# A recommender tower on one core: another order for the first chunks, rotation loads of 120 partitions, rows stored five times

## The reference, cut to what matters

```python
e = jnp.stack([tbl_f[ids[:, f]] for f in range(39)], axis=1)        # (512, 39, 16)
x0 = xk = e
for idx, (W, b) in enumerate(params):                                # W: (39, fk, 128), fk = 39, 64, 64
    z = relu(jnp.einsum('bhd,bkd,hks->bsd', x0, xk, W) + b[None, :, None])
    if idx != 2:
        xk = z[:, :64, :]; direct.append(z[:, 64:, :])
    else:
        direct.append(z)
z = jnp.sum(jnp.concatenate(direct, axis=1), axis=-1)                # (512, 256)
h = concat([z, dense_ctx], 1); h = relu(h @ W_top1 + b_top1); h = relu(h @ W_top2 + b_top2)
y = h @ W_top3
```

## Time and profile before

| | us |
|---|---|
| median of 3 runs (704.96 to 708.79) | 708.59 |
| profiled execution, its own time | 708.69 |
| span of the profiled execution | 706.9 |
| PE busy | 635.9 (90%) |
| DVE busy | 601.0 (85%) |
| POOL busy | 351.6 (50%) |
| ACT busy | 244.8 (35%) |
| DMA, share of 16 engines, SP's queue | 60.7% |

### The profile page before, as it was taken

How to read it: one execution, slowest core, us unless ns; L and a number is a source line. 1 busy time by engine, 2 the same in 40 slices (tenths; PEclk the granted TensorE clock), 3 DMA queues, 4 the chain that set the end, 5 groups by cost and what they waited for, 6 DMA issues and landing times.

```text
span 706.9 us, 5986 instructions
## 1 busy us (share of the span) xinstructions
PE 635.9 (90%) x1856; PEld 347.7 (49%) x1856; DVE 601.0 (85%) x548; ACT 244.8 (35%) x315; POOL 351.6 (50%) x391
## 2 busy tenths in 40 slices
PE   0142679999999999999999999999999999999998
PEld 0020335555555555555555555555555555555544
DVE  0220768999999999999999999999999999999920
ACT  0210242434434434343443334344344343432312
POOL 6765045374756657464746464747566222132210
PEclk9985698999999999999999999999999999999999
DMA  8587087959586776859494949494867668070100
GB/s 204 102 295 168 12 225 230 279 146 251 157 231 194 165 258 143 286 127 301 106 316 89 302 103 278 128 265 142 232 194 189 228 150 275 30 268 1 61 0 0
DMA packets 95118, 126.05 MB, mean 178 GB/s; under 512 B 30312, under 2 KB 38222, under 8 KB 95087
## 3 DMA queue, kind: packets, MB, share of 16 engines
q1 hardware_dynamic: 87935, 124.32, 60.7%
q0 software_dynamic: 5120, 1.32, 2.3%
q10 hardware_dynamic: 2032, 0.04, 0.2%
HBM read 123.09 MB, written 6.39 MB: 183 GB/s over the span
## 4 chain that ended last, share of the span: by engine, by line
PE 83%; DMA 7%; DVE 4%; SPq 3%; issue 1%; POOL 1%; ACT 1%; DVEq 0%; ACTq 0%
PE z L575 53%; PE z L565 9%; PE z L566 8%; PE z L567 8%; DMA rot<-fields 3%; DMA bc<-fields 2%; DVE low L491 1%; POOL emb L309 1%; DMA fields<-xt 1%; DVE whole L515 1%; DVE raw L507 1%; PE z L582 1%; PE z L583 1%; PE z L635 1%; SPq L241 1%
## 5 line engine op out<-in xcount | busy, mean ns | idle before, releaser
L575 PE MATMUL z<-whole,w 128*128 128x512 f32 (+2 forms) x928 | 433.4, 600 | 31.2 <-DVE whole L515 30.4
L575 PEld LDWEIGHTS z<-whole,w 128*128 128x128 f32 (+2 forms) x928 | 177.0, 192 | 188.0 <-issue 172.1
L388 ACT ACTIVATE high<-raw 128x1024 fp32r<-128x1024 f32 (+1 forms) x128 | 135.3, 1058 | 363.4 <-DVE raw L507 312.0
L515 DVE TENSOR_TENSOR whole<-bc,xk 128x1024 f32<-128x1024 f32 (+1 forms) x208 | 229.6, 1127 | 6.7 <-issue 2.4
L309 POOL DMA_INDIRECT emb<-in_tables,rows_all x160 | 194.9, 1218 | 54.1 <-issue 52.9
L491 DVE TENSOR_TENSOR low<-raw,high 128x1024 fp32r<-128x1024 f32 (+1 forms) x128 | 162.0, 1266 | 0.7 <-ACT high L388 0.7
L565 PE MATMUL z<-high,w_high 128*128 128x512 f32 (+1 forms) x256 | 141.8, 554 | 19.2 <-DVE low L491 19.1
L507 DVE TENSOR_TENSOR raw<-bc,xk 128x1024 f32<-128x1024 f32 x112 | 135.5, 1210 | 0.0
L327 POOL TENSOR_TENSOR stack<-stack_raw,stack 64x512 fp32r<-64x512 f32 x32 | 44.6, 1393 | 180.5 <-ACT stack L395 179.6
L566 PE MATMUL z<-high,w_low 128*128 128x512 f32 (+1 forms) x256 | 102.6, 401 | 0.0
L567 PE MATMUL z<-low,w_high 128*128 128x512 f32 (+1 forms) x256 | 102.4, 400 | 0.0
(11 more groups left out here) (52 smaller groups left out, 162.3 us busy)
## 6 DMA issues: line engine op xcount, KB each, us to landing
bc<-fields SPq DMA_DIRECT2D x64, 1024.0 KB, 8.5
rot<-fields SPq DMA_DIRECT2D x32, 390.0 KB
bc<-fields SPq DMA_DIRECT2D x16, 768.0 KB
rot<-fields SPq DMA_DIRECT2D x48, 156.0 KB
rot<-fields SPq DMA_DIRECT2D x16, 312.0 KB
bc<-fields SPq DMA_DIRECT2D x32, 128.0 KB
rep<-fields SPq DMA_DIRECT2D x48, 78.0 KB
fields<-fields SPq DMA_DIRECT2D x16, 234.0 KB
```

The lines of the kernel that those rows point to most:

```text
L388: act.activation(high[0:m, k % PART_SLOTS], raw[0:m, k % RAW_SLOTS], ACT.Copy).then_inc(high_ready, 1)
L515: nc.vector.tensor_tensor(whole[0:rows, n % WHOLE_SLOTS, 0:len(tiles)], left, right, ALU.mult).then_inc(whole_ready, 1)
L575: ins = nc.tensor.matmul(z[layer][:, :], w[layer][0:m, WHOLE_AT[layer, t], :], whole[0:m, k % WHOLE_SLOTS, u], start=(t == 0), stop=(layer ...
```

## The change

The steps are listed in another order for the first chunks, and PE's transposes, ACT's turns, POOL's folds and SP's stores and loads are written out for them by hand. From (0, 3) on the list is the same as before. A rotation is 40 rows instead of 39 (TURN); row 40 is the first row of the next, and its weights are zero. As 40 rows further on is one row further on modulo 39, partition p of tile t reads row 3t + p, and one DMA of 120 partitions loads what three of 39 loaded. All five copies of the block are written from `xt`, the DRAM to DRAM copy is gone; the rotations wait for four copies and the broadcasts for the fifth. For chunk 0, SP issues copies 0 and 2, ACT copies 1 and 3 at the same time, and SP copy 4 after the rotations. `base` is loaded from ACT's queue, and ACT's copy of the dense columns comes ahead of the first `turned`.

```diff
-ROWS0 = ROT_PER_TILE * FIELDS
-LAST0 = (ROT - (T0 - 1) * ROT_PER_TILE) * FIELDS
+TURN = FIELDS + 1
+ROWS0 = ROT_PER_TILE * TURN
+LAST0 = (ROT - (T0 - 1) * ROT_PER_TILE) * TURN
...
-WRITTEN = 2
-COPIES = 3
+TIMES = 5
+FOR_ROT = 4
-STORES = 3 * WRITTEN
+STORES = 3
...
-        PHASES = range(-2, CHUNKS)
+        PHASES = range(1, CHUNKS)
-        STEPS = [(layer, p + 2 - layer) for p in PHASES for layer in range(3) if p + 2 - layer in IN]
+        STEPS = [(0, 0), (1, 0), (0, 1), (2, 0), (0, 2), (1, 1)]
+        STEPS += [(layer, p + 2 - layer) for p in PHASES for layer in range(3) if p + 2 - layer in IN]
...
+        def store_rows(queue, c, n):
+            head = PART // DIM
+            rest = (GATHERS - head) * DIM
+            turns = GATHERS * N
+            signal = stored if n < FOR_ROT else stored_last
+            to = c * CHUNK_ROWS + n * FIELDS * N
+            queue.dma_start(bass.AP(fields.tensor, to, [[SUB, PART], [turns, BY], [1, SUB]]),
+                            xt[:, 0, :].rearrange("p (f b) -> p f b", b=SUB)).then_inc(signal, 16)
+            queue.dma_start(bass.AP(fields.tensor, to + head * N, [[SUB, rest], [turns, BY - 1], [1, SUB]]),
+                            xt[0:rest, 1, 0:(BY - 1) * SUB].rearrange("p (f b) -> p f b", b=SUB)).then_inc(signal, 16)
+            queue.dma_start(bass.AP(fields.tensor, to + (FIELDS - 1) * N, [[SUB, DIM], [1, SUB]]),
+                            xt[0:DIM, 1, (BY - 1) * SUB:PART]).then_inc(signal, 16)
...
-            sp.dma_start(base[:, :], A["base"]).then_inc(ids_in, 16)
...
             def store(c):
                 sp.wait_ge(xt_ready, 2 * (c + 1))
-                for n in range(WRITTEN):
...
-                sp.wait_ge(stored, (c + 1) * 16 * STORES)
+                for n in range(TIMES):
+                    store_rows(sp, c, n)
+                sp.wait_ge(stored, (c + 1) * 16 * STORES * FOR_ROT)
...
                 for r in range(ROT_PER_TILE):
-                    src = bass.AP(fields.tensor, at, [[N, FIELDS], [1, N]])
-                    sp.dma_start(rep[r * FIELDS:(r + 1) * FIELDS, :], src).then_inc(rot_first, 16)
+                    src = bass.AP(fields.tensor, at, [[N, TURN], [1, N]])
+                    sp.dma_start(rep[r * TURN:(r + 1) * TURN, :], src).then_inc(rot_first, 16)
                 for first, last, arrived in ((0, GT, rot_first), (GT, T0, rot_rest)):
-                    for r in range(ROT_PER_TILE):
-                        tiles = len(range(r + first * ROT_PER_TILE, min(ROT, last * ROT_PER_TILE), ROT_PER_TILE))
-                        src = bass.AP(fields.tensor, at + (first * ROT_PER_TILE + r) * N, [[N, FIELDS], [ROT_PER_TILE * N, tiles], [1, N]])
-                        sp.dma_start(rot[r * FIELDS:(r + 1) * FIELDS, first:first + tiles, :], src).then_inc(arrived, 16)
-            def copy_rows(c):
...
+                    src = bass.AP(fields.tensor, at + first * ROT_PER_TILE * N, [[N, ROWS0], [ROT_PER_TILE * N, last - first], [1, N]])
+                    sp.dma_start(rot[:, first:last, :], src).then_inc(arrived, 16)
...
-            store(0)
             load_rotations(0)
-            copy_rows(0)
-            for p in PHASES:
-                if p == -2:
-                    load_broadcasts(0)
-                if p + 3 in IN:
-                    store(p + 3)
-                    copy_rows(p + 3)
-                    load_rotations(p + 3)
-                if p >= -1 and p + 2 in IN:
-                    load_broadcasts(p + 2)
+            store_rows(sp, 0, 4)
+            load_broadcasts(0, range(2))
+            store(1)
+            load_broadcasts(0, range(2, SECTIONS))
+            load_rotations(1)
+            load_broadcasts(1)
+            store(2)
+            load_rotations(2)
+            for c in range(3, CHUNKS + 1):
+                if c in IN:
+                    store(c)
+                    load_rotations(c)
+                load_broadcasts(c - 1)
```

The line `store(0)` becomes `sp.wait_ge(xt_ready, 2)`, `store_rows(sp, 0, 0)`, `store_rows(sp, 0, 2)` and a wait for the four copies. POOL and ACT:

```diff
             gather(0)
             gather(1)
+            gather(2)
+            landed(2)
+            fold(0, 0)
+            stack_part(1, 0)
+            own_done()
+            gather(3)
+            landed(3)
+            fold(1, 0)
+            fold(0, 1)
+            stack_part(2, 0)
+            own_done()
+            gather(4)
+            landed(4)
+            stack_part(1, 1)
+            fold(0, 2)
+            fold(1, 1)
...
+            act.dma_start(base[:, :], A["base"]).then_inc(ids_in, 16)
...
+            act.wait_ge(dense_t, 1)
+            act.activation(denseT[:, :], top[0][0:DENSE, :], ACT.Copy).then_inc(dense_ready, 1)
             turned(0)
+            act.wait_ge(xt_ready, 2)
+            store_rows(act, 0, 1)
+            store_rows(act, 0, 3)
...
+            turned(1)
+            for g in SPLIT[0]:
+                high_part(0, 0, g)
+            layer0_out(0)
+            for g in SPLIT[1]:
+                high_part(1, 0, g)
+            stack_part(1, 0)
+            layer1_direct(0)
+            layer1_kept(0)
+            turned(2)
+            for g in SPLIT[0]:
+                high_part(0, 1, g)
+            layer0_out(1)
+            for g in SPLIT[2]:
+                high_part(2, 0, g)
+            stack_part(2, 0)
+            for g in SPLIT[0]:
+                high_part(0, 2, g)
+            high_part(1, 1, SPLIT[1][0])
+            turned(3)
+            for g in SPLIT[1][1:]:
+                high_part(1, 1, g)
+            stack_part(1, 1)
+            layer0_out(2)
+            layer1_direct(1)
+            layer1_kept(1)
```

More of the change, by code:

```diff
@@ L28 @@
 LAST = T1 - 1
-WRITTEN = 2
-COPIES = 3
-LINES = (WRITTEN + COPIES) * FIELDS
+TIMES = 5
+FOR_ROT = 4
+LINES = TIMES * FIELDS
 GT = 2
@@ L148, in tower @@
         stored = sem("stored")
-        copied = sem("copied")
+        stored_last = sem("stored_last")
         rot_first = sem("rot_first")
@@ L189, in tower @@
         STACK_NO = {x: n for n, x in enumerate(x for x in STEPS if x[0])}
-        FOLD_NO = {x: n for n, x in enumerate(
-            x for p in range(-2, CHUNKS + 1) for x in ((2, p - 1), (0, p + 2), (1, p + 1)) if x[1] in IN)}
+        FOLDED = [(0, 0), (1, 0), (0, 1), (0, 2), (1, 1)]
+        FOLDED += [x for p in range(1, CHUNKS + 1) for x in ((2, p - 1), (0, p + 2), (1, p + 1)) if x[1] in IN]
+        FOLD_NO = {x: n for n, x in enumerate(FOLDED)}
         PART_AT = {(layer, t): n for n, (layer, t) in enumerate((m, t) for m in range(3) for t in split_tiles(m))}
@@ L234, in load_rotations, with load_broadcasts @@
                 for r in range(ROT_PER_TILE):
-                    src = bass.AP(fields.tensor, at, [[N, FIELDS], [1, N]])
-                    sp.dma_start(rep[r * FIELDS:(r + 1) * FIELDS, :], src).then_inc(rot_first, 16)
+                    src = bass.AP(fields.tensor, at, [[N, TURN], [1, N]])
+                    sp.dma_start(rep[r * TURN:(r + 1) * TURN, :], src).then_inc(rot_first, 16)
                 for first, last, arrived in ((0, GT, rot_first), (GT, T0, rot_rest)):
-                    for r in range(ROT_PER_TILE):
-                        tiles = len(range(r + first * ROT_PER_TILE, min(ROT, last * ROT_PER_TILE), ROT_PER_TILE))
-                        src = bass.AP(fields.tensor, at + (first * ROT_PER_TILE + r) * N, [[N, FIELDS], [ROT_PER_TILE * N, tiles], [1, N]])
-                        sp.dma_start(rot[r * FIELDS:(r + 1) * FIELDS, first:first + tiles, :], src).then_inc(arrived, 16)
-            def copy_rows(c):
[L245 to L250, removed]
+                    src = bass.AP(fields.tensor, at + first * ROT_PER_TILE * N, [[N, ROWS0], [ROT_PER_TILE * N, last - first], [1, N]])
+                    sp.dma_start(rot[:, first:last, :], src).then_inc(arrived, 16)
+            def load_broadcasts(c, sections=range(SECTIONS)):
                 at, b = c * CHUNK_ROWS, c % 2
-                sp.wait_ge(copied, 16 * (c + 1))
+                sp.wait_ge(stored_last, (c + 1) * 16 * STORES)
                 if c == 1:
@@ L256, in load_broadcasts @@
                     sp.wait_ge(w_low_ready, 2)
-                for n in range(SECTIONS):
+                for n in sections:
                     first, end = SECTION * n, min(LAST, SECTION * (n + 1))
@@ L265, in load_broadcasts @@
                     sp.dma_start(bc[b][:, first:end, :], src).then_inc(bc_in[b][n], 16)
+                if SECTIONS - 1 not in sections:
+                    return
                 if c >= 2:
@@ L348, in _ @@
             gather(1)
-            for p in range(-2, CHUNKS + 1):
+            gather(2)
[14 more added lines that the diff above has]
+            fold(1, 1)
+            for p in range(1, CHUNKS + 1):
                 if p + 4 in IN:
@@ L353, in _ @@
                     landed(p + 4)
-                if p - 1 in IN:
-                    fold(2, p - 1)
+                fold(2, p - 1)
                 if p + 1 in IN:
@@ L377, in turned @@
                 if c:
-                    act.wait_ge(stored, c * 16 * STORES)
```

(24 more changed lines are left out.)

19 lines of the change are left out of this document (6 added, 13 removed).

## The result

The changed kernel takes 697.41 us in the median (697.3 to 698.07, 4 runs), the kernel before 707.17 on the same chip: a ratio of 0.9852, 95% interval [0.9828, 0.9875]. It is 1.5% faster and inside the range of 675 to 699. But the gain is 9.8 us in the medians and 11.4 us in the profiled executions (708.69 to 697.30), where 21.4 were forecast.

A forecast was written before the change was run, and what follows sets the result against it. PE and DVE were taken to bound the kernel, with DVE's early idle recoverable: 25.5 us against 44.5 and a start 2.4 us sooner, 21.4 us less, gives 687.3 us from 708.69. Range 675 to 699 (own range 680 to 694).

The forecast's parts named there:

- The reading: Beginning, up to step (0,3): DVE's idle time, 44.5 us before, sets the gain; the long middle costs nothing.
- signs of being wrong: DVE idle in the middle, rotation waits in (0,1), or a first product later than 31 us.
- The first rows: Chunk 0's start: first store at 20.1, copies landed and rotations issued near 24.6, first product at 29.8, 2.4 us sooner.
- The rotation loads: Chunk 0's load of 120 partitions runs at 359 GB/s; everything landed 8.6 us after the first issue.
- the other bound: Lower bound for the rate of a 120-partition load: 187 GB/s, that of the old rotation loads.
- The first rival: Loads of 120 partitions run like the old ones, 187 GB/s, so rotations take 12.8 us: 696 us; chance 0.14.
- The handoffs: DVE's waits on other engines in the first steps, such as 8.4 us for `xk` and 3.5 in (0,1).
- The slot wait in (1,0): Step (1,0): DVE waits 2.2 us for a `whole` slot while PE is still at half clock.
- The rival in which they cost nothing: Idle of 3.5, 2.2, 3.7 and 2.3 us from orders on ACT and SP vanishes: 675.6 us; chance 0.18.
- (0,3) starting near 117: Sign of the forecast: step (0,3), which started at 140.73 before, starts near 117 us.
- The slower rival: Fifteen small stores per chunk land over 10.2 us late, so chunks from 4 on wait; about 733 with 14; chance 0.05.

The follow-up runs named there:

- the edits of ACT's order: New order, rotation loads of 128 partitions, plus three edits: chunk 2 turned later, chunk 1's layer 0 output later, chunk 3 turned earlier; 685.32 us, ratio 0.9680 to the kernel before.
- the slower one with the old order: The kernel before with only the new data path: 40 rows, one load of 120 partitions, five stores on SP, no copy; 710.19 us, ratio 1.0041.

## Why the prediction was right in direction and half right in size

**The reading** held. DVE's idle time in the beginning was the account, the middle stayed full, and start and waits together give 11.0 of the 11.4 us gained. Against the forecast 10.4 us are missing (21.4 - 11.0): 1.3 at the first product, 10.0 in rotation waits, less 0.9 in the handoffs. The prediction's own signs of being wrong came too: a first product later than 31 (31.15), and a rotation wait in (0,1).

**The first rows.** The first store was issued at 20.44 instead of 20.1, and the four copies took 2.2 us to land after the last issue, not 1.5: rotations at 25.69 instead of 24.6. With 0.3 us more for tiles 0 and 1 this gives back 1.3 us of the 2.4.

**The rotation loads** are the step that failed. "I take 383 x 120/128 = 359, since its shape is nearly that of the broadcast": from 29 to 36 us it was 208 GB/s on average, near the other bound. The 10.0 us are here: rotation waits behind the first product were forecast at 2.2 + 3.7 = 5.9 us and were 5.04 + 1.37 + 0.37 + 3.42 + 0.81 + 4.86 = 15.9. Loads of 128 partitions put them at 5.2 and the time at 687.05, against the 687.3 forecast. So near a hit is partly luck: in that kernel's profiled execution (684.9) all idle time behind the first product is 22.3 us, not 25.5. The row nearest in shape was the wrong guide, and so was the scaling by engine count, which gave the same 359. The first rival had this mechanism, at 0.14. That its 696 is so near the 697.41 is partly luck as well: it put 4.2 us at chunk 0, 4.2 at chunk 3 and up to 0.6 at chunk 1, while against the forecast the trace has 3.1 more at chunk 0 (0.3 of them ahead of the first product), 2.0 at chunk 3, 1.4 at chunk 1 and 3.8 at chunk 2, where the rival had nothing.

One term of the working was wrong without an effect on this: 20 rotations of 78 KB are 1560 KB, not 1638. The old loads move 1.84 MB, and at 187 GB/s the lead before data flows is 3.0 us instead of 2.5.

**The second term behind it** is at chunk 2. Forecast: rotations there at 86, no wait. `xt` was ready at 72.8, but SP was still issuing the broadcasts of chunk 1 until 74.7. Its fifteen store issues then took 13.2 us (74.74 to 87.97) while these loads ran; three of them took 1.8 to 2.6 us. The rotations were complete at 100.25. With nothing in front (chunk 3) fifteen issues took 7.4 us. The longest issue:

```profile
81.93 2.59 SPq L218 DMA_DIRECT2D fields<-xt  x1
```

With loads of 128 partitions chunk 2 still stores for 12 us, but the slack covers it. Chunk 1 shows the same overlap that the working left out: its rotations, forecast for 60.8, were complete at 70.01, as the broadcasts issued right behind them ran at the same time (DMA share 1.04 to 1.07 from 58 to 70 us).

**The handoffs** sum as forecast, though not each: 18.7 us of idle apart from rotations, where 19.6 were worked out. The slot wait in (1,0) never came (2.2), `high` in (0,1) cost 0.8 instead of 3.5, while (2,0) cost 4.5 instead of 2.2 and (1,1) 1.7 instead of nothing. The rival in which they cost nothing is refuted by the traces: with the loads mended DVE still idles 2.3 us for `high` in (0,1), 3.3 in (2,0), 2.6 for the rotations of chunk 3 and 2.9 behind (0,3), 11.1 in all where 11.7 were forecast, and the time is 687.05 and not 675.6. What taking them away would be worth stays open, since the edits of ACT's order didn't shorten them in sum. The sign "(0,3) starting near 117" didn't fit the working, which has its rotations at 114.2; it started at 122.85.

**Order and stores.** The order, with the edits ahead of the first product, carries the gain, as shown by the kernel that has nothing else of the change. The slower rival's mechanism, small stores that land too late in every chunk, did not show: from 140 to 640 us DVE worked 498.3 us in the changed kernel and 498.1 in the slower one with the old order (1.0041), whose loss is issue time in the beginning.

## What to carry to other kernels

When a load changes its number of partitions, its price isn't to be had from the nearest shape: time it alone, with one or two counts beside it. Here 128 partitions, 8 of them unused, beat 120 by 2.1 to 2.5 us a load and 9 to 10 us a kernel. In a fill phase, count each engine's idle time up to the first step that both orders share. And price issues by what still runs ahead of them: here the same store issue took 0.51 us with nothing in front and up to 2.59 us behind running loads.

## What the hardware showed that was not expected

Loads of 120, 104 and 88 partitions take 7.6 to 8.5 us for 5 tiles of 2 KB rows, nearly the same for 0.90 as for 1.23 MB. These are the counts that would give 8 partitions each to 15, 13 and 11 engines; the division is inferred. 117 partitions take 5.6 to 5.8, and 128 take 5.4 to 6.3. Three loads of 39 take 9.0 to 9.4, so going from these to one load of 120 could gain only about 0.8 to 1.4 us per chunk.
